# Rotary embedding of a second attention layer: on GpSimd, from a copy that ScalarE makes of queries and keys

## The reference

```python
x = x + attn(layernorm(x))     # 32 heads of 32, 8 kv heads, sign weights
x = x + xattn(layernorm(x))    # read, attention with rope, write, gated mlp, write
x = x + ffn(layernorm(x))      # dense 1024x1024 with low-rank adapters
```

```python
qkv_in = rat_read(h, ...)            # einsum 'blhc,hoc->bloh', layer norm of 256 features, gain, bias; o = q, k, v
q, k, v = (einsum(qkv_in_o, qkv_w[o]) for o in range(3))   # 256 -> 256, 16 heads of 16
def rope(x, pos):                    # half = 8, for q and k
    x1, x2 = x[..., :half], x[..., half:]
    return concatenate([x1 * cos - x2 * sin, x2 * cos + x1 * sin])
p = softmax(where(mask, rope(q) @ rope(k).T / sqrt(16), -1e30)); o = p @ v
```

## Time and profile before

| | us |
|---|---|
| median of 3 runs | 971.18 |
| lowest, highest | 969.48, 979.40 |
| the profiled execution | 975.68 |
| its span, first to last instruction | 973.7 |
| share of busy time, TensorE, VectorE, ScalarE, GpSimd | 87%, 68%, 42%, 31% |

### The profile page before, as it was taken

One profiled execution on the slowest core, in us unless ns is written; L12 is line 12 of the kernel. 1 busy time (PEld: TensorE's weight loads), 2 busy tenths in 40 slices (PEclk: granted clock), 3 DMA queues, 4 the chain that ended last, 5 costly groups with the idle time before them and its releaser, 6 DMA issues.

```text
span 973.7 us, 15022 instructions
## 1 busy us (share of the span) xinstructions
PE 842.3 (87%) x5594; PEld 454.4 (47%) x5594; DVE 658.1 (68%) x1364; ACT 409.1 (42%) x795; POOL 304.9 (31%) x297
## 2 busy tenths in 40 slices
PE   3899689999999998888967779737699999999977
PEld 2574232433433433455644223225656656656643
DVE  7865457888888873577775857044578769779761
ACT  4555416767666766032322456513323323323310
POOL 2000005766777677010000335321222222223110
PEclk8999899999999999999986787558599999999997
DMA  8665522222313231202227231110001011011011
GB/s 332 238 209 149 156 70 86 80 71 86 92 59 106 61 103 39 98 10 70 54 75 285 53 99 41 56 24 12 1 1 45 1 43 44 0 43 33 1 40 47
DMA packets 75625, 75.78 MB, mean 78 GB/s; under 512 B 37493, under 2 KB 63877, under 8 KB 74918
## 3 DMA queue, kind: packets, MB, share of 16 engines
q1 hardware_dynamic: 74998, 68.77, 23.0%
q10 hardware_dynamic: 560, 6.12, 1.6%
HBM read 53.56 MB, written 21.04 MB: 77 GB/s over the span
## 4 chain that ended last, share of the span: by engine, by line
PE 65%; DVE 14%; ACT 7%; DMA 4%; SPq 4%; issue 4%; POOL 2%; POOLq 0%; DVEq 0%; ACTq 0%; PEldq 0%
PE psum L1955 7%; PE psum L1536 6%; PE psum L1618 6%; PE psum L1892 5%; PE psum L1669 5%; PE psum L1658 5%; PE psum L1726 4%; PE psum L1733 4%; PE psum L1877 3%; PE psum L1679 3%; PE psum L1826 3%; PE psum L1940 2%; DMA ops<-q_scr 2%; PE psum L1804 2%; SPq L527 2%
## 5 line engine op out<-in xcount | busy, mean ns | idle before, releaser
L1211 DVE TENSOR_REDUCE m_neg<-psum 128x1 f32<-128x512 f32 x256 | 164.4, 682 | 43.8 <-PE psum L1618 41.6
L880 ACT ACTIVATE region_x<-psum 128x512 f32<-128x512 f32 x256 | 140.8, 596 | 63.5 <-PE psum L1658 63.3
L670 POOL TENSOR_TENSOR region_p<-region_x 128x2048 f32<-128x2048 f32 x32 | 145.3, 4539 | 41.4 <-ACT region_x L880 25.6
L1618 PE MATMUL psum<-ops 96*128 96x512 f16 x256 | 96.5, 385 | 12.0 <-DMA ops<-q_scr 10.8
L1658 PE MATMUL psum<-ops 98*128 98x512 f16 x256 | 95.7, 381 | 1.8 <-ACT region_x L880 1.7
L1536 PE MATMUL psum<-region_x,region_w 128*128 128x512 f16 x320 | 77.6, 400 | 3.0 <-ACT region_w L818 3.0
L1955 PE MATMUL psum<-ynT,region_w 128*128 128x128 f32 x512 | 63.7, 289 | 6.3 <-ACT ynT L1036 6.3
L1618 PEld LDWEIGHTS psum<-ops 96*128 96x128 f16 x256 | 24.7, 97 | 92.3 <-DVE m_neg L1211 63.5
L1669 PE MATMUL psum<-region_x,v_g 128*32 128x512 f32 x512 | 67.8, 604 | 0.0
L1955 PEld LDWEIGHTS psum<-ynT,region_w 128*128 128x128 f32 x512 | 62.1, 204 | 10.1 <-ACT ynT L1036 10.1
L1726 PE MATMUL psum<-sign_o_all,region_a 128*128 128x512 f16 x256 | 58.5, 379 | 4.3 <-DVE region_p L1279 2.8
(11 more groups left out here) (218 smaller groups left out, 1495.9 us busy)
## 6 DMA issues: line engine op xcount, KB each, us to landing
ops<-q_scr SPq DMA_DIRECT2D x48, 128.0 KB, 2.6
region_a<-in_x SPq DMA_DIRECT2D x8, 512.0 KB, 8.5
region_a<-in_w_q SPq DMA_DIRECT2D x8, 512.0 KB, 6.6
region_w<-in_w_o SPq DMA_DIRECT2D x8, 512.0 KB, 4.0
region_w<-in_kern SPq DMA_DIRECT2D x16, 256.0 KB, 2.8
kern_scr<-region_w SPq DMA_DIRECT2D x32, 128.0 KB, 1.9
region_p<-in_x SPq DMA_DIRECT2D x8, 512.0 KB, 3.6
region_a<-kern_scr ACTq DMA_DIRECT2D x1, 4096.0 KB
```

Source lines behind the costliest of these rows:

```text
L670: pool.tensor_tensor(pair_sum[:, n], prob_a[:, 2 * n], prob_a[:, 2 * n + 1], ALU.add).then_inc(pair_ready, 1)
L880: act.activation(prob_a[:, kt, j, :], psum[:, (0, 4, 5)[(16 * i + n) % 3], :], ACT.Exp, scale=A_SCALE).then_inc(p_ready, 1)
L1211: dve.tensor_reduce(m_neg[:, i % 3, n:n + 1], psum[:, 1 + (16 * i + n) % 3, :], AX_X, ALU.max, negate=True).then_inc(s_max, 1)
L1618: pe.matmul(psum[:, 1 + (16 * i + n) % 3, :], qa_op[u][0:A_MAX, j, qt * P:(qt + 1) * P], k_op[u][0:A_MAX, :], start=True, stop=True).then_ ...
```

## The change

The six operations of the rotation move from VectorE's list to GpSimd's. GpSimd doesn't read PSUM here, so ScalarE copies bank 6 (128x512) to `qk_sb` behind the copy of the values, and GpSimd waits for `qk_copied`. `qk_sb` and `rope_a` lie in `region_w`, which is free then; `rot` stays in `yn`. On GpSimd `rope(i - 1)` stands ahead of `read_root(i)`, and the last one, `rope(7)`, ahead of the causal selections. On VectorE `read(i)` follows what stood before the rotation, and the four maxima after the loop no longer stand behind `rope(7)`.

```diff
-        rope_a = yn[:, 2 * H:3 * H]
+        rope_a, qk_sb = region_w[:, 2 * H:3 * H], region_w[:, 0:2 * H]
...
+            def rope(i):
+                pool.wait_ge(qk_copied, i + 1)
+                qk = qk_sb.rearrange("p (h e f) -> p h e f", e=2, f=HALF)
+                to = rot.rearrange("p (h e f) -> p h e f", e=2, f=HALF)
+                other = rope_a.rearrange("p (h f) -> p h f", f=HALF)
+
+                def angle(k):
+                    return trig[:, k, i:i + 1, :].broadcast_to([P, 2 * X_NH, HALF])
+
+                for e in range(2):
+                    pool.tensor_tensor(to[:, :, e, :], qk[:, :, e, :], angle(1), ALU.mult).then_inc(rope_step, 1)
+                for e in range(2):
+                    pool.tensor_tensor(other, qk[:, :, 1 - e, :], angle(0 if e else 2), ALU.mult).then_inc(rope_step, 1)
+                    pool.wait_ge(rope_step, 6 * i + 9 + 2 * e)
+                    pool.tensor_tensor(to[:, :, e, :], to[:, :, e, :], other, ALU.add).then_inc(rope_step, 1)
+                    pool.wait_ge(rope_step, 6 * i + 10 + 2 * e)
...
+            pool.wait_ge(trig_done, 4)
             for i in range(NT):
+                if i > 0:
+                    rope(i - 1)
                 read_root(i)
...
+            rope(NT - 1)
...
                 act.activation(v_x[:, i, :].rearrange("p (h e) -> p h e", e=32)[:, :, 0:X_HD],
                                psum[:, 7, 0:H].rearrange("p (h e) -> p h e", e=X_HD), ACT.Copy).then_inc(vx_ready, 1)
+                act.activation(qk_sb, psum[:, 6, :], ACT.Copy).then_inc(qk_copied, 1)
...
             for i in range(NT):
-                if i > 0:
-                    rope(i - 1)
                 read(i)
...
             x_max_lo(0)
-            rope(NT - 1)
             for m in range(4):
                 x_maximum(1, m)
```

More of the change, by code:

```diff
@@ L338, in build_program @@
         ynT_mm, ynT_ready, qkv_mm = sem("ynT_mm"), sem("ynT_ready"), sem("qkv_mm")
-        rope_step, vx_ready, rT_mm, r_hi, r_lo, qk_stored = (sem(n) for n in (
-            "rope_step", "vx_ready", "rT_mm", "r_hi", "r_lo", "qk_stored"))
+        rope_step, vx_ready, qk_copied, rT_mm, r_hi, r_lo, qk_stored = (sem(n) for n in (
+            "rope_step", "vx_ready", "qk_copied", "rT_mm", "r_hi", "r_lo", "qk_stored"))
         xq_loaded = [sem(f"xq_loaded{u}") for u in range(4)]
@@ L1313, in read @@
                                           mv3[:, o, 0:1], rs3[:, o:o + 1], ALU.subtract, ALU.mult).then_inc(yn_ready, 1)
[L1315 to L1330, removed]
             def split(i):
```

## The result

| | kernel before | changed kernel |
|---|---|---|
| median of 4 runs each, us | 971.07 | 994.19 |
| lowest, highest | 969.48, 979.40 | 993.46, 996.11 |
| profiled execution, its span | 975.68, 973.7 | 994.37, 992.6 |

A forecast was written before the change was run, and what follows sets the result against it. The prediction took the chain of waits through the rotation, not busy shares, to bound the second attention's tile loop. Terms 6.4 + 0 + 1.0 + 1.5 + 6.0 = +14.9 us on 971.2 gave 986 us, range 974 to 997.

The forecast's parts named there:

- Start of the rotation: Each tile: GpSimd waits for ScalarE's value copy and 128x512 copy, so it starts 0.97 us later than VectorE did.
- Six operations: The rotation on GpSimd: 0.70 us per operation, 4.4 us per tile, against 0.42 us per operation on VectorE.
- A steady round: Rounds 1 to 5: TensorE's queue delays the transposes of `yn`, +1.28 us a round, +6.4 us in all.
- The path over the root: Steady rounds: rotation, then root on GpSimd, then `yn` on VectorE; 0.97 us later, less than TensorE's path.
- The clock: Rounds 1 to 5: a 2.85 us TensorE gap brings lower-clock spells in four of five rounds, 1.5 us each, +6.0 us.
- Round 6: Tile 5's rotation: product to `yn` stays 6.31 us, VectorE's freed time being eaten by GpSimd; 0 us.
- Round 7 and tail: Round 7: 5.35 us becomes 6.31, +1.0; after the loop, tile 7's rotation to its low part's maxima, +1.5 us.
- The sum: Whole kernel: steady rounds 6.4, round 6 0, round 7 1.0, tail 1.5, clock 6.0; +14.9 us.
- Rival 1: Rounds 1 to 5: no lower-clock spell follows the new TensorE gap; +8.9 us, 980 us; chance 0.25.
- Rival 2: GpSimd is quicker than its nearest row, 3.3 to 3.6 us a rotation; 971 to 974 us; chance 0.10.
- Rival 3: GpSimd slower: 5.3 us a rotation, 995 us, chance 0.13; with VectorE locking it out, 8.7 us, 1020 us, chance 0.05.
- Rival 4: Faster: VectorE's queue sets the round and loses 2.49 us a tile; up to -20 us, 951 us; chance 0.02.

The follow-up runs named there:

- e2: Changed kernel with the transposes of the rotated tile behind 15 instead of 4 projection matmuls on TensorE; 1.0191 of the kernel before.
- e7: Changed kernel with the rotated tile in its own room, root first, transposes at round end, tile 7 on VectorE, loads reordered, fill; 1.0076 of the kernel before.
- e4: Changed kernel without the last two of GpSimd's six rotation operations, so four of six and part of the computation left out; 0.9951 of the kernel before.
- e6: Changed kernel with ScalarE's two copies in the other order, queries and keys before values; 1.0123 of the kernel before, median 990.7 us.

## Why the prediction was right, and where its terms were off

The direction, slower by over 1%, and its mechanism were right: the rotation stands on the chain and gets longer there, TensorE's next work waits for it, and no busy share shows that. 986 us was forecast with a range from 974 to 997, 994.2 measured. In the loop 14.9 us were forecast and 12.7 measured, and that nearness is in part luck, as the terms show.

- **Start of the rotation.** 0.97 us after VectorE's old start was forecast, 0.95 measured.
- **Six operations.** 0.70 us each and 4.4 together forecast; 0.717 to 0.722 and 4.46 to 4.49 measured. The row of the same shape, 0.727, was the right one to take, and against it neither the runs of 8 elements nor the broadcast table cost anything. By the Trainium skill, GPSIMD Engine Reference, section 4.1, a factor of about two against VectorE was to be had; the trace shows 0.72 against 0.42, 1.7.
- **A steady round.** +1.28 forecast, +1.08 to +1.10 measured. TensorE was done with the 12 matmuls and free for the transposes of `yn` 1.30 us later in relation to the copy, as forecast (at 435.50 after; before, they started at 478.14). But the six of them and the eight of the next tile's layer norm then took 1.54 us, to 437.04, and 1.75 before, to 479.89, where TensorE came from a gap:

```profile
478.85 1.04 PE L1733 MATMUL psum<-ident,region_p 128*128 128x128 f32 x8
```

The term left this out: 1.30 less 0.21 is the 1.09. (The ends of matmuls are modelled, so only the sum is firm: the last transpose ends 9.16 us after the copy before and 10.25 after.) The path over the root was nearly as long, 1.05 us later than before and not the 0.97 that I had: moving TensorE's own (e2) won nothing.
- **The clock.** Forecast: a spell in four of five rounds, 1.5 us each, +6.0. Measured: two of five, 1.44 each, +2.9. The gap was 2.88 to 2.90 us every time, and the runs don't show why one is followed by a spell and the next is not. The size of a spell held, its frequency was mis-sized.
- **Round 6.** 0 forecast, +1.45 measured. With the clock kept up in both kernels it was +0.10. My sum of waits was right, and the clock term was missing here: I had counted spells in rounds 1 to 5 alone, although already showed a falling clock at the start of round 6 (0.95 over 490.4 to 504.8; the round itself runs from 499.4 to 518.4, with a mean of 0.64).
- **Round 7 and tail.** +1.0 and +1.5 forecast; +1.35 and +1.56 measured, +1.06 and +2.32 without clock and stores.
- **The sum.** +14.9 forecast for the loop, 12.7 measured. The misses, 3.1 too much for the spells of rounds 1 to 5, 1.0 too much in the steady rounds and 1.8 too little in rounds 6 and 7, partly cancel. That is luck.
- **Outside the loop.** Nothing forecast, and +6.2 us in the profile: 1.8 in front of it, and 4.4 behind it. Of these, 1.7 lie in one group of the second attention (11.7 us against 10.0), 1.7 in one round of the write (37.6 us against 35.9) and 0.8 at the end. The same steps of 1.7 us come in other numbers in other profiles; the four-of-six kernel, faster than before, has three such rounds. Whether the change makes them more frequent is open: the profiles are too few. The four runs of the kernel before were also on the fast side of its later ones.

Rival 1 (the clock holds) was half true. Rival 2 fell with the 0.72. Rival 3's lockout appeared only in e7, where the rotation was moved beside VectorE's two-input operations. Rival 4 is answered by e4: a rotation of 2.97 us gained, and the full one takes 4.47 here.

## What to carry to other kernels

Before work is moved to an idle engine, count the way there: the copy that the engine needs took 0.95 us on the chain and made half the loss in the loop. Operations that are 1.7 times slower added little where other work lay beside them, and most of their extra length where none did, in the tail. Ask what waits for the result and in which queue; a result that is needed at once belongs on the engine that reads its source directly. If a wait leaves TensorE idle for two to three us, price the clock as well, in every round and not in the steady ones alone.

## What the runs showed of the hardware

- A wait of TensorE can be paid again afterwards by the lower level: 20 unread matmuls in each of rounds 6 and 7 of the kernel before brought round 6 from 18.96 to 15.40 us and round 7 from 16.42 to 13.65, once the loads had been moved (the moved loads alone left them at 19.03 and 16.45). A gap of 2.88 us was followed by a spell in two of five rounds, one of 2.62 in three of five (e6), one of 2.12 in two of five (e2), and one of 1.64 in none.
- A 32 KB store landed after 14.35 us when a 4 MB load on another engine's queue was issued 0.3 us behind it, and two smaller loads just before; with the three moved away the last store on the chain took 1.91. A faster stretch can move a transfer into a collision that the slower one avoided.
- GpSimd's 128x256 addition took 0.716 us alone and up to 1.708 beside a VectorE operation with two SBUF inputs, which itself took 1.44 us instead of 1.23. The Trainium skill, SBUF — State Buffer, section SBUF: two separate sides, states that of two such operations the one that starts first keeps the shared ports and the other waits. The trace agrees: both grew, by 1.0 and 0.2 us.
